# A mixture of experts in a graph network's kernel: experts and combine as one stage, with sixteen experts' slots combined first and partial rows kept in DRAM

## What is computed

```python
def _L0_ffn_ref(x, phi, scale, w1, b1, w2, b2):
    xn = _l2norm(x, axis=2)
    phin = scale * _l2norm(phi, axis=0)
    logits = jnp.einsum('bld,des->bles', xn, phin)
    d_w = jax.nn.softmax(logits, axis=-1)
    c_w = jax.nn.softmax(logits.reshape(b, l, E * S), axis=-1)      # E = S = 32
    slots = jnp.einsum('bld,bles->besd', xn, d_w)                   # d = 768
    h = jax.nn.gelu(jnp.einsum('besd,edh->besh', slots, w1) + b1[:, None, :], approximate=False)   # h = 384
    eo = jnp.einsum('besh,ehd->besd', h, w2) + b2[:, None, :]
    eo = eo.reshape(b, E * S, d)
    return jnp.einsum('bkd,blk->bld', eo, c_w)
...
x = x + _L0_gnn_ref(_layernorm(x, axis=-1), ...)
x = x + _L0_ffn_ref(_layernorm(x, axis=-1)[None], ...)[0]
```

## Time and profile before

| | us |
|---|---|
| median of 3 runs (lowest, highest) | 3882.11 (3880.23, 3882.63) |
| the profiled execution: its time | 3876.24 |
| the profiled execution: its span, from the first to the last instruction | 3874.2 |
| TensorE busy | 3261.8 (84% of the span) |
| VectorE busy | 1975.7 (51%) |
| ScalarE busy | 1092.4 (28%) |
| GpSimd busy | 1819.5 (47%) |
| moved by DMA | 994.13 MB, 257 GB/s on the mean |

### The profile page before, as it was taken

How to read it: one execution, slowest core, us unless ns; L and a number is a source line. 1 busy time by engine, 2 the same in 40 slices (tenths; PEclk the granted TensorE clock), 3 DMA queues, 4 the chain that set the end, 5 groups by cost and what they waited for, 6 DMA issues and landing times. The chain is left out here.

```text
span 3874.2 us, 63864 instructions
## 1 busy us (share of the span) xinstructions
PE 3261.8 (84%) x20859; PEld 1862.9 (48%) x20859; DVE 1975.7 (51%) x2924; ACT 1092.4 (28%) x1313; POOL 1819.5 (47%) x1693
## 2 busy tenths in 40 slices
PE   2202699999999999978999999999999964469998
PEld 2201355555555556544555555555555521136665
DVE  8977333333333333325777777777777750021111
ACT  3634122222222222213434434343443420011110
POOL 0010676666766766637666666666666500000000
PEclk9999799999999999989999999999999987789999
DMA  8124788888888888839888888888888729934443
GB/s 342 73 107 191 246 306 290 288 285 284 292 285 285 292 287 285 288 133 337 314 300 291 301 295 297 298 294 298 295 298 305 270 100 368 333 135 154 150 149 124
DMA packets 265455, 994.13 MB, mean 257 GB/s; under 512 B 38306, under 2 KB 67260, under 8 KB 265200
## 3 DMA queue, kind: packets, MB, share of 16 engines
q0 software_dynamic: 133728, 656.12, 49.0%
q1 hardware_dynamic: 131472, 334.56, 24.3%
HBM read 867.64 MB, written 122.89 MB: 256 GB/s over the span
## 5 line engine op out<-in xcount | busy, mean ns | idle before, releaser
L1135 POOL DMA_INDIRECT m_ring<-table,idx x833 | 923.0, 1108 | 498.7 <-PE m_part L1296 256.6
L868 POOL DMA_INDIRECT a_ring<-table,idx x833 | 880.9, 1058 | 434.3 <-PE a_part L972 213.8
L1296 PE MATMUL m_part<-m_ring,m_pick 128*128 128x512 f16 (+1 forms) x3332 | 597.6, 328 | 15.8 <-DMA m_ring<-table,idx 13.6
L972 PE MATMUL a_part<-a_ring,a_pick 128*128 128x512 f16 (+1 forms) x3332 | 579.9, 328 | 10.3 <-DMA a_ring<-table,idx 9.8
L1296 PEld LDWEIGHTS m_part<-m_ring,m_pick 128*128 128x128 f16 x3332 | 323.6, 98 | 242.7 <-issue 31.8
L1311 PE MATMUL m_ps_s<-m_dw,m_xn 128*128 128x512 f16 x1764 | 429.7, 381 | 11.9 <-DVE slots L1194 11.9
L972 PEld LDWEIGHTS a_part<-a_ring,a_pick 128*128 128x128 f16 x3332 | 323.1, 98 | 219.8 <-issue 20.0
L1622 PE MATMUL c_po<-c_eh,c_cT 128*128 128x512 f16 (+1 forms) x1568 | 328.6, 327 | 12.6 <-DVE c_cT L1591 12.6
L1324 PE MATMUL m_ps_l<-phi_h,m_xT 128*128 128x512 f16 x1176 | 309.8, 379 | 0.3
L1311 PEld LDWEIGHTS m_ps_s<-m_dw,m_xn 128*128 128x128 f16 x1764 | 171.8, 98 | 195.6 <-issue 19.4
L952 PE MATMUL a_ps_o<-W2h,a_vT 128*128 128x512 f16 (+1 forms) x1176 | 248.2, 327 | 0.9 <-ACT a_vT L897 0.9
(11 more groups left out here) (353 smaller groups left out, 4427.0 us busy)
## 6 DMA issues: line engine op xcount, KB each, us to landing
e_w1s<-in_L_ffn_w_dram SPq DMA_DIRECT2D x32, 1152.0 KB, 14.8
e_w2s<-in_L_ffn_w_dram SPq DMA_DIRECT2D x32, 1152.0 KB, 14.0
cw_dram<-m_cst SPq DMA_DIRECT2D x49, 512.0 KB
c_cw<-cw_dram SPq DMA_DIRECT2D x49, 512.0 KB, 4.7
x_pad<-xs SPq DMA_DIRECT2D x7, 2688.0 KB, 23.9
table<-stage SPq DMA_DIRECT2D x49, 384.0 KB, 2.3
a_own<-table SPq DMA_DIRECT2D x49, 384.0 KB, 4.0
table<-a_stage SPq DMA_DIRECT2D x49, 384.0 KB, 2.8
```

Source lines behind the costliest of these rows:

```text
L868: pool.indirect_dma_start(out=ring[:, t, :], out_offset=None, in_=table, in_offset=bass.IndirectOffsetOnAxis(ap=idx[:, k:k + 1], axis=0)). ...
L972: mm = nc.tensor.matmul(part[:, bass.ds(to + a, z - a)], pick[:, i % 2, t, :], ring[:, t, half * D + a:half * D + z], start=False, stop=(t ...
L1135: pool.indirect_dma_start(out=ring[:, t, :], out_offset=None, in_=table, in_offset=bass.IndirectOffsetOnAxis(ap=idx[:, n:n + 1], axis=0)). ...
L1296: mm = nc.tensor.matmul(part[:, bass.ds(off + at, e - f)], pick[:, i % 2, t, :], ring[:, n % RING, half * D + f:half * D + e], start=False ...
```

## The change

`experts` and `combine` become one stage, `mixture`. The slots are halved: the first 16 experts (groups 0 to 3, `HG` = 4) and the other 16 (groups 4 to 7). The work of a bin is halved in the same way into units (bin, half), of which there are 98: a unit loads half of a bin's weights (256 KB, for which `second_layer` now writes each row of `cw_dram` as high and low part of the first half, then of the second), makes 8 transposes and 24 matmuls.

The order is: the experts of groups 0 to 3; scale and split of their `eo`; units 0 to 27, the first half of the bins 0 to 27 (`EARLY` = 28), whose partial rows ScalarE scales and SP stores in `part_dram` (384 KB each); units 28 to 55, the second half of the same bins, for which SP loads x and the partial row (`pb`, one buffer, 384 KB) and VectorE adds the two before it adds the product; units 56 to 97, both halves of the bins 28 to 48 in turn. The experts' groups 4 to 7 are made between the products of units 2 to 22: up product at unit 2, 8, 14 and 20, transposes one unit later, down product two units later. Their matrices and biases are loaded on POOL's queue, which begins when the last w2 of group 3 has landed. The scale of the second half is worked out at units 23 to 26. All loops are written out. The copy of the slots with its scaling is gone: the up product reads `slots`, and the factor is in the operation that adds the bias. `hb`, the biases and the products' PSUM tile are single now. No barrier stands between the two parts.

```diff
+    part_dram = nc.dram_tensor("part_dram", (NBR * P, D), F32).ap()
...
-        with ExitStack() as late:
-            eo = late.enter_context(nc.sbuf_tensor("eo", [P, KC, D], F32))
-            experts(nc, w1, eb1, w2, eb2, slots, eo, ident16)
-            combine(nc, eo, cw_dram, x2_dram, ident16, out)
+        mixture(nc, w1, eb1, w2, eb2, slots, cw_dram, part_dram, x2_dram, ident16, out)
...
-                        nc.scalar.activation(cst[:, 0:K], lg[:, :], ACT.Copy, scale=rZ[:, 0:1]).then_inc(cw_hi, 1)
+                        nc.scalar.activation(by_half(cst)[:, :, 0, :], lg[:, :].rearrange("p (h k) -> p h k", h=2), ACT.Copy, scale=rZ[:, 0:1]).then_inc(cw_hi, 1)
...
-                        v.scalar_tensor_tensor(cst[:, K:2 * K], lg[:, :], rZ[:, 0:1], cst[:, 0:K], ALU.mult, ALU.subtract).then_inc(cw_lo, 1)
+                        v.scalar_tensor_tensor(by_half(cst)[:, :, 1, :], lg[:, :].rearrange("p (h k) -> p h k", h=2), rZ[:, 0:1], by_half(cst)[:, :, 0, :],
+                                               ALU.mult, ALU.subtract).then_inc(cw_lo, 1)
...
-def experts(nc, w1, eb1, w2, eb2, slots, eo, ident16):
-def combine(nc, eo, cw_dram, x2_dram, ident16, out):
+def mixture(nc, w1, eb1, w2, eb2, slots, cw_dram, part_dram, x2_dram, ident16, out):
...
+        HG = NG // 2
+        HK = KC // 2
+        EARLY = 28
+        units = [(b, 0) for b in range(EARLY)] + [(b, 1) for b in range(EARLY)] + [(b, h) for b in range(EARLY, NBR) for h in range(2)]
+        NU = len(units)
+        up_at = {2 + 6 * g: HG + g for g in range(HG)}
+        turn_at = {k + 1: g for k, g in up_at.items()}
+        down_at = {k + 2: g for k, g in up_at.items()}
+        MAX_AT = max(down_at) + 1
+        SCALE_AT = MAX_AT + 1
+        HIGH_AT = SCALE_AT + 1
+        LOW_AT = HIGH_AT + 1
...
+        def free_product(eng, k):
+
+            if 0 <= k < EARLY:
+                eng.wait_ge(act_done, k + 1)
+            elif k >= EARLY:
+                eng.wait_ge(dve_done, dve_count(k))
...
+        def load_up(eng, g):
+            wait(eng, up, g - 1)
+            for q in range(G):
+                eng.dma_start(w1s[:, G * (g % 2) + q], w1_v[:, g * G + q:g * G + q + 1, :, :].rearrange("p o c h -> p (o c) h")).then_inc(w1_in[g // HG][G * (g % 2) + q], 16)
+
+        def load_down(eng, g):
+            wait(eng, down, g)
+            for q in range(G):
+                eng.dma_start(w2s[:, q], w2_v[:, g * G + q:g * G + q + 1, :, :].rearrange("p o c h -> p (o c) h")).then_inc(w2_in[g // HG][q], 16)
...
+                load_up(sp, 0)
+                for g in range(HG):
+                    if g + 1 < HG:
+                        load_up(sp, g + 1)
+                    load_bias1(sp, g)
+                    load_down(sp, g)
+                    load_bias2(sp, g)
+                for k in range(NU + 2):
+                    if k < NU:
+                        b, h = units[k]
+                        wait(sp, cw_turned, k - 1)
+                        sp.dma_start(cw[:, k % 2, :], cw_dram[b * P:(b + 1) * P, h * K:(h + 1) * K]).then_inc(cw_in[k % 2], 16)
+                        if (b < EARLY) == (h == 1):
+                            if b >= 2:
+                                sp.wait_ge(dve_done, last_use(b - 2))
+                            sp.dma_start(xb[:, b % 2, :], x2_dram[b * P:(b + 1) * P, :]).then_inc(x_in[b % 2], 16)
+                        if b < EARLY and h == 1:
+                            sp.wait_ge(stored[b % 2], 16 * (b // 2 + 1))
+                            wait(sp, summed, b)
+                            sp.dma_start(pb[:, :], part_dram[b * P:(b + 1) * P, :]).then_inc(p_in, 16)
+                    j = k - 2
+                    if j >= 0 and j in ob_of:
+                        b, h = units[j]
+                        o = ob_of[j]
+                        if h == 0:
+                            sp.wait_ge(act_done, j + 1)
+                            sp.dma_start(part_dram[b * P:(b + 1) * P, :], ob[:, o % 2, :]).then_inc(stored[o % 2], 16)
+                        else:
+                            sp.wait_ge(dve_done, dve_count(j))
+                            rows = TAIL if b == NBR - 1 else P
+                            sp.dma_start(out[b * P:b * P + rows, :], ob[0:rows, o % 2, :]).then_inc(stored[o % 2], 16)
...
+                for q in range(G):
+                    pool.wait_ge(w2_in[0][q], 16 * HG)
+                load_up(pool, HG)
+                load_bias1(pool, HG)
+                load_up(pool, HG + 1)
+                load_down(pool, HG)
+                load_bias2(pool, HG)
+                pool.wait_ge(maxed, 1)
+                pool.partition_all_reduce(am[:, 0:1], mx[:, 0:1], P, bass.bass_isa.ReduceOp.max).then_inc(allmax, 1)
+                for g in range(HG + 1, NG):
+                    load_bias1(pool, g)
+                    if g + 1 < NG:
+                        load_up(pool, g + 1)
+                    load_down(pool, g)
+                    load_bias2(pool, g)
+                pool.wait_ge(maxed, 2)
+                pool.partition_all_reduce(am[:, 1:2], mx[:, 1:2], P, bass.bass_isa.ReduceOp.max).then_inc(allmax, 1)
...
+                def high(half):
+                    act.wait_ge(scaled, half + 1)
+                    nc.scalar.activation(eh[:, HK * half:HK * (half + 1), :], eo[:, :, :], ACT.Copy, scale=sc[:, half:half + 1]).then_inc(e_hi, 1)
+
+                def high_back(k):
+                    act.wait_ge(cw_turned, k + 1)
+                    wait(act, prod, k - 1)
+                    nc.scalar.activation(cT[:, k % 2, 0, :], ps_t[:, 0, 0:K // 2], ACT.Copy).then_inc(hi_back, 1)
+
+                for g in range(HG):
+                    gelu(g)
+                    hidden(g)
+                high(0)
+                high_back(0)
+                for k in range(NU):
+                    if k in up_at:
+                        gelu(up_at[k])
+                    if k in turn_at:
+                        hidden(turn_at[k])
+                    if k == HIGH_AT:
+                        high(1)
+                    if k + 1 < NU:
+                        high_back(k + 1)
+                    if k < EARLY:
+                        act.wait_ge(prod, k + 1)
+                        wait(act, stored[k % 2], 16 * (k // 2))
+                        nc.scalar.activation(ob[:, k % 2, :], ps_o[:, k % 2, 0:D], ACT.Copy, scale=inv[:, 0:1]).then_inc(act_done, 1)
...
+                def low_back(k):
+                    v.wait_ge(cw_turned, k + 1)
+                    wait(v, prod, k - 1)
+                    v.tensor_copy(cT[:, k % 2, 1, :], ps_t[:, 1, 0:K // 2]).then_inc(lo_back, 1)
...
+                for k in range(NU):
+                    b, h = units[k]
+                    if k in up_at:
+                        hidden_bias(up_at[k])
+                    if k in down_at:
+                        expert_out(down_at[k])
+                    if k == MAX_AT:
+                        largest(1)
+                    if k == SCALE_AT:
+                        scale(1)
+                    if k == LOW_AT:
+                        low(1)
+                    if k + 1 < NU:
+                        low_back(k + 1)
+                    if k < EARLY:
+                        continue
+                    if b < EARLY:
+                        v.wait_ge(x_in[b % 2], 16 * (b // 2 + 1))
+                        v.wait_ge(p_in, 16 * (b + 1))
+                        v.tensor_tensor(xb[:, b % 2, :], xb[:, b % 2, :], pb[:, :], ALU.add).then_inc(summed, 1)
+                        v.wait_ge(summed, b + 1)
+                    else:
+                        v.wait_ge(x_in[b % 2], 16 * (b // 2 + 1))
+                    v.wait_ge(prod, k + 1)
+                    if k in ob_of:
+                        o = ob_of[k]
+                        wait(v, dve_done, dve_count(k) - 1)
+                        wait(v, stored[o % 2], 16 * (o // 2))
+                        v.scalar_tensor_tensor(ob[:, o % 2, :], ps_o[:, k % 2, 0:D], inv[:, h:h + 1], xb[:, b % 2, :], ALU.mult, ALU.add).then_inc(dve_done, 1)
+                    else:
+                        v.scalar_tensor_tensor(xb[:, b % 2, :], ps_o[:, k % 2, 0:D], inv[:, h:h + 1], xb[:, b % 2, :], ALU.mult, ALU.add).then_inc(dve_done, 1)
...
+                turn_weights(0)
+                for k in range(NU):
+                    if k in up_at:
+                        up_product(up_at[k])
+                    if k in turn_at:
+                        turn(turn_at[k])
+                    if k in down_at:
+                        down_product(down_at[k])
+                    if k + 1 < NU:
+                        turn_weights(k + 1)
+                    product(k)
```

More of the change, by code:

```diff
@@ new lines, in mixture @@
+        w2_in = [[sem(f"w2_in{half}_{q}") for q in range(G)] for half in range(2)]
+        b1_in = [sem(f"b1_in{half}") for half in range(2)]
+        b2_in = [sem(f"b2_in{half}") for half in range(2)]
+        cw_in = [sem(f"cw_in{q}") for q in range(2)]
```

(72 more changed lines are left out.)

288 lines of the change are left out of this document (77 added, 211 removed).

## The result

The changed kernel takes 3937.64 us (median of 4 runs, 3935.65 to 3939.48), the kernel before beside it 3881.17 (4 runs, 3878.26 to 3882.63): ratio 1.0146, with 95% between 1.0129 and 1.0164. It is slower by 56 us, inside the range given and 23 us under the forecast. The profiled execution has a span of 3933.8 us, 59.6 more than before.

What follows compares the result with a forecast made beforehand. `experts` was taken as bound by transfers, `combine` by TensorE. First product at 3344.5, plus 175, 213, 210 and 10.6, gave 3953 us of span, 79 more; added to the median, 3961 us, 2% slower, range 3905 to 4005.

Steps and rivals of the forecast that it cites:

- w2 of the first half landed: End of the first four groups' loads: 111.2 us of bytes at 361 GB/s plus start and buffer wait, landing at 3291.0.
- from there to the first product: After that landing: 45.5 us of POOL's transfers, 0.4 of reduction, 7.6 of scale and split; first product at 3344.5.
- units 0 to 27: First halves of early bins: 121.7 us of units, 31.8 of expert work, 17 of late loads and smaller terms; 175 us.
- units 28 to 55: Second halves of early bins: a loop through VectorE's sum and SP's queue takes 7.6 us a unit, 213 us in all.
- units 56 to 97: Last 21 bins: weights stand behind the store of the second half before, 10.0 us a bin instead of 8.69; 210 us.
- POOL's transfers: Twenty transfers ahead of POOL's reduction, priced half fixed and half by contiguous piece: 45.5 us, holding the reduction 38 us.
- Rival 1: POOL's transfers cost a flat 1.11 us each, as its gathers do: 23 us less, 3938 us; 18 in 100.
- the 1.9 us added for the matrices' traffic: Units 0 to 27: weights land 1.9 us later with matrices in flight, making the loss 3.1 instead of 1.2 us a pair.
- The pieces of expert work: Units 0 to 27: twelve units have expert work covering the load's wait; the other 16 lose 0.6 or 1.55 us each.
- the loop I named: Units 28 to 55: sum, partial row, store, weights, landing, transposes, copy, next sum; 7.6 us against 4.35 of TensorE's work.
- Rival 3: Units 28 to 55: TensorE's clock falls to its lower level, 8.7 us a unit, at most 31 us more; 12 in 100.
- Rival 4: Loads land sooner than taken: 1.5 us less gives today's time, 2.0 us less gives 3865; 6 in 100.

Runs made afterwards that it cites:

- e9: Changed kernel with six weight buffers, two partial-row buffers and POOL's reduction ahead of its last twelve transfers; ratio 0.9795 to the kernel before.
- e4: Changed kernel loading only a sixth of each w1 and a third of each w2 in groups 5 to 7; span 3903.3 us, ratio from one run not given.
- e3: Changed kernel with two buffers for partial rows, so SP waits for the sum of the unit before the last; one run, 3924.4 us.
- e1: Changed kernel with the weights of unit k+1 asked for at the head of SP's turn k; 3834.16 us, ratio 0.9887 to the kernel before.
- e5: Changed kernel with six weight buffers laid over dead slots, weights asked for up to five units ahead, one partial-row buffer; ratio 0.9869 to the kernel before.
- e10: e9 with the up products of groups 4 to 7 at units 5, 10, 15 and 20; ratio 0.9803 to the kernel before.
- e12: e9 with up products at units 5, 11, 17 and 23 and `EARLY` = 30; ratio 0.979 to the kernel before.

## Why the prediction was right, and what in it was wrong

The direction and the main cause were right, at 50 in 100: a load's steps don't halve with its bytes, and they no longer fit under half the work. By the prediction's terms, on the span:

| term | predicted | measured |
|---|---|---|
| w2 of the first half landed | 3291.0 | 3295.4 |
| from there to the first product | 53.5 | 23.2 |
| units 0 to 27 | 175 | 197 |
| units 28 to 55 | 213 | 206.5 |
| units 56 to 97 | 210 | 200.7 |
| tail | 10.6 | 10.9 |
| span | 3953 | 3933.8 |

- **Up to the landing:** right to 4.4 us in 120.
- **POOL's transfers, the step that failed:** "I take half of the 1.108 us as fixed and half by the piece: ... = 45.5 us" measured 13.8. Rival 1's price, that of a gather for each (22 us), was too high as well. A plain transfer from POOL costs less than a gather, and neither SP's queue nor a count of pieces says how much: 768 pieces take 0.85 us, 384 take 0.75, 32 take 0.5. SP, which takes 2.1 us for 768 pieces, was the wrong row to lean on. Here the Trainium skill, "DMA: Bandwidth & Descriptors", section "Anatomy of one DMA — SWDGE (gpsimd) path", was the better guide: it calls the generation of descriptors small, and these rows agree. And e9 shows that a wait on POOL was not even worth its own length, since the matrices of group 4 were next.
- **Units 0 to 27, mis-sized:** the mechanism, a load under two units of work, was right; the 1.9 us added for the matrices' traffic was not. e4 gives the size of that term: 6.6 us of landing on the mean with the whole matrices, 3.7 with a sixth and a third of them, 2.9 apart. And it does not fall on all loads alike. The chain of the changed kernel has the long ones:

```profile
3329.07 12.21 DMA e_cw<-cw_dram
3347.18 10.02 DMA e_cw<-cw_dram
3363.11 11.74 DMA e_cw<-cw_dram
```

  They fall in the stretches in which POOL's matrices of 1152 KB are under way: the long landings are those of the weights of units 3 to 8, 11 to 14, 19 and 20. The pieces of expert work were to cover the wait. Those of groups 5 to 7 hardly do: the next matrices are asked for when such a piece has freed their buffer, so they are under way in the units between the pieces. Of the nine pieces only one, the down product of group 5 at 3392.5, has a long landing beside it; the loads beside the other eight take 2.9 to 4.0 us.
- **Units 28 to 55:** predicted 7.6 us a unit; measured 7.1 to 7.8, and once 9.4. Of the loop, the step "partial row, store, weights, to the landing", 5.4 us, measured 5.2, and SP was released in 0.07 instead of 0.17 us. What the prediction did not have is the second loop at 6.9 us. It changed nothing here, but it means that the loop I named was not worth 85 us by itself: e3 took it away and won 13. TensorE's busy share, said to be near 0.57, was 0.70 (147.26 of 210.90 us): products at the low clock are longer, beside the loop.
- **Units 56 to 97:** 10.0 us a bin predicted, 9.56 measured. The chain has bins of 10.3 and 9.1 us in turn: product 3.91, 1.03 of scaling, 0.34 of store, then a landing of 4.19 or 3.03. The mechanism stood; the landings were unevenly shorter.
- **Rival 3, the low clock:** the granted clock fell, to 0.92 in the middle part, not to the lower level throughout, and cost little: of some 28 transposes in the chain of that part four took 1.02 or 1.03 us, the others 0.62 to 0.67. e3 shows where it costs more.
- **Rival 4, the loads land sooner:** no. The Trainium skill, "DMA: Bandwidth & Descriptors", the same section, gives 2.6 us for 256 KB by its fit, which is made for transfers issued on POOL; these are issued on SP. The shortest `e_cw` of 98 took 2.9 us, the median 4.2 and the longest 13.5. In e1 the shortest took 2.4, so the fit is neither the usual time nor a floor.

The errors of the terms, in the order of the table, are +4.4, -30.3, +22, -6.5, -9.3 and +0.3 us, together -19. The good total owes much to luck: without the +22 of the first units it would have been 41 us off. It is luck too that the time met rival 1's number, 3938: its price for POOL's transfers was wrong by 8 us.

## What to carry to other kernels

When a unit of work is cut in half, list the steps of its load that don't halve (the wait ahead of it in the queue, the issue, the landing) and compare their sum with the new unit, for every loop that closes through a buffer: behind the one you find there may be another, almost as long, and removing one buys only the difference. On an in-order queue, put loads that need nothing ahead of instructions that wait; here that alone turned 1.5% slower into 1.1% faster, and six weight buffers in dead memory, with a second one for partial rows, into 2.1% faster. Before you shorten a wait, see what arrives next for the same engine: a wait in front of a later arrival is free.

## What the runs showed of the hardware that was not expected

- A small load beside megabyte transfers lands late by far more than its share of the bytes: in the changed kernel's first part 12 of 26 loads of 256 KB took 9.3 to 12.2 us and the others 2.9 to 4.0; none took over 6.5 when those transfers were cut to a sixth and a third (e4).
- POOL issues a plain transfer of a w1 matrix (1152 KB in 768 pieces) in 0.85 us, SP in 2.1 us.
- One chip (that of e5 to e9) ran the kernel before at about 4147 us at one time and at about 3879 us at another; two others took 4143 to 4156 us (e10 to e12). The difference lay ahead of the mixture, in the stages with gathers: a stretch of 1400 us in e12 moves 247 GB/s at a clock of 0.92, where the changed kernel had moved 274 at 0.98. The kernel before showed it beside each of them, so pairs stay comparable. Its cause is open; no run was made for it.
